# A gated delta-rule layer in chunks of 16 tokens on one core: the first half's errors return in one transfer, its sums are stored in two parts, gates and betas are stored behind them

## What is computed

```python
def step(S, inp):
    qt, kt, vt, at, bt = inp
    err = jnp.einsum('bhij,bhj->bhi', S, kt) - vt
    S = at[..., None] * S - bt[..., None, None] * (err[..., None] * kt[:, :, None, :])
    o = jnp.einsum('bhij,bhj->bhi', S, qt)
    return (S, o)
```

## Time and profile before

| | |
|---|---|
| median of 3 runs | 7554.44 us (7550.18 to 7566.12) |
| the profiled execution | 7551.86 us, span of its instructions 7550.1 us |
| the 64 slots | the first 24 of 40 slices of the span; 56 of them from 508.1 us to 4391.0 us |
| busy in these slots (1500 to 2500 us) | DVE 81%, POOL 72%, PE 63%, ACT 45%, DMA engines 65% |
| the second stage | from about 4570 us on |

### The profile page before, as it was taken

One profiled execution on the slowest core, in us unless ns is written; L12 is line 12 of the kernel. 1 busy time (PEld: TensorE's weight loads), 2 busy tenths in 40 slices (PEclk: granted clock), 3 DMA queues, 4 the chain that ended last, 5 costly groups with the idle time before them and its releaser, 6 DMA issues. The chain is left out here.

```text
span 7550.1 us, 176117 instructions
## 1 busy us (share of the span) xinstructions
PE 5140.1 (68%) x58695; PEld 3396.8 (45%) x58695; DVE 5425.1 (72%) x16005; ACT 3324.8 (44%) x7234; POOL 3635.1 (48%) x4232
## 2 busy tenths in 40 slices
PE   5666666666666666666666643777778777777777
PEld 4554444455554454454454542333433333433333
DVE  6888878888888788878788874555666556665665
ACT  4444444444444444444444432444444444444444
POOL 4777767767767767767767772111111111111110
PEclk8777777777777777777777766888888888888888
DMA  4766666665666666666666651111121111111111
GB/s 118 160 154 140 145 155 134 146 157 133 145 152 138 144 152 139 147 151 138 144 151 140 147 134 50 48 47 45 45 50 45 42 42 42 42 45 42 42 42 35
DMA packets 1172894, 786.82 MB, mean 104 GB/s; under 512 B 1039923, under 2 KB 1091795, under 8 KB 1157844
## 3 DMA queue, kind: packets, MB, share of 16 engines
q1 hardware_dynamic: 864468, 583.96, 34.0%
q10 hardware_dynamic: 307712, 193.48, 10.7%
HBM read 473.80 MB, written 303.50 MB: 103 GB/s over the span
## 5 line engine op out<-in xcount | busy, mean ns | idle before, releaser
L465 POOL TENSOR_TENSOR qp<-qp,pt 128x512 f32<-128x512 f32 (+7 forms) x1024 | 1049.5, 1025 | 85.5 <-issue 5.2
L827 DVE SCALAR_TENSOR_TENSOR p_bank<-y,conv_w,p_bank 128x128 f32<-128x128 f32 x3072 | 826.2, 344 | 241.0 <-ACT p_bank L658 222.2
L524 PE MATMUL p_bank<-st 64*32 64x80 f32 x16384 | 508.3, 292 | 614.4 <-issue 452.8
L460 POOL TENSOR_TENSOR qp<-qp,ab 128x512 f32<-128x512 f32 (+7 forms) x1024 | 864.9, 845 | 75.3
L1684 DVE TENSOR_REDUCE nmax<-w_bank 128x1 f32<-128x512 f32 x1024 | 637.4, 682 | 338.0 <-PE w_bank L1310 330.0
L1265 POOL TENSOR_TENSOR ot<-ot,ln_w 128x1024 f32<-128x1024 f32 x64 | 150.6, 2352 | 1407.5 <-ACT ot L1540 1407.5
L524 PEld LDWEIGHTS p_bank<-st 64*32 64x32 f32 x16384 | 451.8, 142 | 674.4 <-issue 672.4
L462 POOL TENSOR_TENSOR pt<-qp,vb 128x512 f32<-128x512 f32 (+7 forms) x1024 | 747.7, 730 | 9.3 <-DVE vb L904 9.3
L497 PE MATMUL d_bank<-xd,kt 32*64 32x128 f32 x7936 | 366.1, 336 | 407.6 <-DVE st L845 407.6
L594 PEld LDWEIGHTS p_bank<-xnT,wqkv 128*128 128x128 f32 x4096 | 537.7, 213 | 160.4 <-issue 160.4
L594 PE MATMUL p_bank<-xnT,wqkv 128*128 128x128 f32 x4096 | 564.6, 299 | 42.6 <-ACT st L671 36.8
(11 more groups left out here) (219 smaller groups left out, 11695.0 us busy)
## 6 DMA issues: line engine op xcount, KB each, us to landing
db<-decay_dram SPq DMA_DIRECT2D x124, 1024.0 KB, 12.3
prod_dram<-prod ACTq DMA_DIRECT2D x64, 1280.0 KB, 7.4
kp<-prod_dram SPq DMA_DIRECT2D x64, 640.0 KB, 6.2
qp<-prod_dram SPq DMA_DIRECT2D x64, 640.0 KB, 7.7
a_dram<-at ACTq DMA_DIRECT2D x64, 512.0 KB
ab<-a_dram SPq DMA_DIRECT2D x64, 512.0 KB, 6.1
v_dram<-vt ACTq DMA_DIRECT2D x64, 512.0 KB
vb<-v_dram SPq DMA_DIRECT2D x64, 512.0 KB, 5.5
```

What stands on the lines that cost most here:

```text
L460: link(nc.gpsimd.tensor_tensor(q, q, ab[:, g, r:r + 1, :].to_broadcast([128, w, DV]), ALU.mult), 1)
L465: link(nc.gpsimd.tensor_tensor(q, q, pt2[:, 0:w], ALU.add))
L524: mm = nc.tensor.matmul(p_bank[b % 2][at_:at_ + 32, ROW * hq:ROW * hq + ROW], slot_[:, DV:DV + 2 * C], slot_[:, 0:ROW], start=True, stop=True)
L827: nc.vector.scalar_tensor_tensor(out=zz, in0=y[:, j % Y_BANKS, i, :, tap:tap + C], scalar=conv_w[:, m, tap:tap + 1], in1=zz, op0=ALU.mult, ...
```

## The change

Four edits. In DRAM the errors now lie as rows of tokens, and the store of the first half writes 128 x 8 runs of 64 numbers into them; one transfer of 128 rows of 1024 numbers brings the whole chunk back into `xe`, second half included. That second half is never written in the loop; it is filled with zeros once, ahead of the loop, from the cleared tile `vt`, and SP and ACT wait for this. `crossed` stores each of its two banks as soon as it is copied. The stores of gates and betas are taken out of `gates` and `betas` and stand behind `crossed` on ACT.

```diff
@@ -165,7 +165,7 @@
     a_dram = [dram(f"a_dram{g}", [C, GB, H, DV]) for g in range(GROUPS)]
     beta_dram = [dram(f"beta_dram{g}", [GB, H, C]) for g in range(GROUPS)]
     upd_dram = [dram(f"upd_dram{g}", [GB, H, C, DV]) for g in range(GROUPS)]
-    e_dram = [dram(f"e_dram{g}", [GB, H, HALF, DV]) for g in range(GROUPS)]
+    e_dram = [dram(f"e_dram{g}", [C, GB, H, DV]) for g in range(GROUPS)]
     x_dram = [dram(f"x_dram{g}", [C, GB, H, DV]) for g in range(GROUPS)]
     decay_dram = [dram(f"decay_dram{g}", [2, GB * HP, DV]) for g in range(GROUPS)]
     x = ins["L0_attn_x"]
@@ -244,7 +244,7 @@
         def conv_bank(j):
             return (p_bank[0], p_bank[1], c_bank)[j % 3][:]
 
-        consts_in = sem("consts_in")
+        consts_in, e_zeroed = sem("consts_in"), sem("e_zeroed")
         ident_done = sem("ident_done")
         init_done = sem("init_done")
         x_in = [sem(f"x_in{g}") for g in range(GROUPS)]
@@ -288,6 +288,11 @@
                 (conv_b[:], ins["conv_b"]),
             ):
                 sp.dma_start(tile, src).then_inc(consts_in, 16)
+
+            sp.wait_ge(init_done, 1)
+            for g in range(GROUPS):
+                sp.dma_start(e_dram[g].rearrange("t b h i -> b t (h i)"), vt[:]).then_inc(e_zeroed, 16)
+            sp.wait_ge(e_zeroed, 16 * GROUPS)
 
             def load_x(n, g):
                 src = x[GB * g:GB * g + GB].rearrange("b (n t) c -> n b t c", t=C)
@@ -330,19 +335,17 @@
                 if valid(lo, hi):
                     sp.wait_ge(solve_chain, SOLVE_OPS * s + FIRST_HALF_OPS)
                     held(sp, sp_passed)
-                    if due(dma_of(xe_in, n, g, -2, 16 * GB)[1]):
-                        sp.wait_ge(*dma_of(xe_in, n, g, -2, 16 * GB))
+                    if due(dma_of(xe_in, n, g, -2)[1]):
+                        sp.wait_ge(*dma_of(xe_in, n, g, -2))
                         held(sp, sp_passed)
-                    sp.dma_start(e_dram[g].rearrange("b h t i -> (b h) t i"), eb[:, 0:HALF]).then_inc(e_wr[g], 16)
+                    sp.dma_start(e_dram[g][0:HALF].rearrange("t b h i -> (b h) t i"), eb[:, 0:HALF]).then_inc(e_wr[g], 16)
                     sp.wait_ge(*dma_of(v_wr, n, g, 0))
                     held(sp, sp_passed)
                     sp.wait_ge(*dma_of(e_wr, n, g, 0))
                     held(sp, sp_passed)
-                    for b in range(GB):
-                        sp.dma_start(xe[C * b:C * b + HALF].rearrange("t (h i) -> t h i", h=H),
-                                     e_dram[g][b].rearrange("h t i -> t h i")).then_inc(xe_in[g], 16)
+                    sp.dma_start(xe[:], e_dram[g].rearrange("t b h i -> b t (h i)")).then_inc(xe_in[g], 16)
                 if valid(lo, hi):
-                    sp.wait_ge(*dma_of(x_wr, n, g, 0))
+                    sp.wait_ge(*dma_of(x_wr, n, g, 0, 32))
                     held(sp, sp_passed)
                     sp.dma_start(xk[:], x_dram[g].rearrange("t b h i -> (b h) t i")).then_inc(xk_in[g], 16)
                 if updates(lo, hi):
@@ -563,7 +566,7 @@
 
             def cross(s, n, g):
 
-                pe.wait_ge(*dma_of(xe_in, n, g, 0, 16 * GB))
+                pe.wait_ge(*dma_of(xe_in, n, g, 0))
                 pe.wait_ge(f_freed, scores_use(s) + 2)
                 for u in range(2):
                     bank = use(cross_use(s), u)
@@ -636,6 +639,7 @@
         def _(act):
             act.wait_ge(consts_in, 16 * 7)
             act.wait_ge(init_done, 1)
+            act.wait_ge(e_zeroed, 16 * GROUPS)
 
             def filled(first, k):
                 act.wait_ge(f_filled, first + k + 1)
@@ -710,20 +714,21 @@
             def crossed(s, n, g):
 
                 act.wait_ge(*dma_of(p_wr, n, g, 0))
-                if due(dma_of(x_wr, n, g, -1)[1]):
-                    act.wait_ge(*dma_of(x_wr, n, g, -1))
+                if due(dma_of(x_wr, n, g, -1, 32)[1]):
+                    act.wait_ge(*dma_of(x_wr, n, g, -1, 32))
+                if due(dma_of(xk_in, n, g, -2)[1]):
+                    act.wait_ge(*dma_of(xk_in, n, g, -2))
                 for u in range(2):
                     bank = filled(cross_use(s), u)
                     nc.scalar.activation(xo[:, 512 * u:512 * u + 512], bank[:], ACT.Copy).then_inc(f_freed, 1)
-                act.wait_ge(f_freed, cross_use(s) + 2)
-                if due(dma_of(xk_in, n, g, -2)[1]):
-                    act.wait_ge(*dma_of(xk_in, n, g, -2))
-                act.dma_start(x_dram[g].rearrange("t b h i -> b t (h i)"), xo).then_inc(x_wr[g], 16)
+                    act.wait_ge(f_freed, cross_use(s) + u + 1)
+                    dst = x_dram[g][:, :, HP * u:HP * u + HP].rearrange("t b h i -> b t (h i)")
+                    act.dma_start(dst, xo[:, 512 * u:512 * u + 512]).then_inc(x_wr[g], 16)
 
             def products(s, n, g):
-                if due(dma_of(x_wr, n, g, -1)[1]):
+                if due(dma_of(x_wr, n, g, -1, 32)[1]):
                     act.wait_ge(*dma_of(p_wr, n, g, -1))
-                    act.wait_ge(*dma_of(x_wr, n, g, -1))
+                    act.wait_ge(*dma_of(x_wr, n, g, -1, 32))
                 for b in range(GB):
                     act.wait_ge(p_filled, 8 * s + b + 1)
                     nc.scalar.activation(prod[:, b, :], p_bank[b % 2][:, 0:4 * ROW], ACT.Copy).then_inc(p_freed, 1)
@@ -744,6 +749,8 @@
                 for j in range(2):
                     bank = filled(front1_use(s), 1 + j)
                     nc.scalar.activation(at[:, 512 * j:512 * j + 512], bank[:], ACT.Sigmoid).then_inc(f_freed, 1)
+
+            def store_gates(s, n, g):
                 act.wait_ge(f_freed, front1_use(s) + 3)
                 if due(dma_of(ab_in, n, g, -2)[1]):
                     act.wait_ge(*dma_of(ab_in, n, g, -2))
@@ -756,6 +763,8 @@
                 nc.scalar.activation(bt[:], bank[0:H, 0:P], ACT.Sigmoid, bias=bb[:]).then_inc(f_freed, 1)
                 act.wait_ge(f_freed, front1_use(s) + 4)
                 nc.scalar.activation(bt[:], bt[:], ACT.Copy, scale=-1.0).then_inc(bneg_done, 1)
+
+            def store_betas(s, n, g):
                 act.wait_ge(bneg_done, s + 1)
                 if due(dma_of(nb_in, n, g, -2)[1]):
                     act.wait_ge(*dma_of(nb_in, n, g, -2))
@@ -782,6 +791,9 @@
                     place_keys(s + 1, 1 - g)
                 if valid(lo, hi):
                     crossed(s, n, g)
+                if ahead:
+                    store_gates(s + 2, n + 1, g)
+                    store_betas(s + 2, n + 1, g)
                 if front:
                     silu(s + 1, 1 - g, 4)
                     silu(s + 1, 1 - g, 5)
```

## The result

| | before | after |
|---|---|---|
| median | 7557.03 us (7544.2 to 7585.56, 7 runs) | 7515.94 us (7498.94 to 7537.36, 7 runs) |
| ratio of after to before | | 0.9934, 95% interval 0.9916 to 0.9953 |
| span of the profiled execution | 7550.1 us | 7514.1 us |

By the ratio the change makes the kernel 0.66% faster; between the medians it is 41 us, where I forecast 79 (7475). The time lies inside the range of 7395 to 7590.

A forecast was written before the change was run, and what follows sets the result against it. A chain of waits once per slot was taken as the bound, no engine being full. 60 x (-1.1 - 0.4) = -90 and +11 for the start gave -79 us: 7475 us, range 7395 to 7590 for 8 in 10.

The forecast's parts named there:

- Term one: Errors return sooner, so PE's wait for them goes and DVE's for `update` shrinks: -1.1 us per slot, between 0 and -1.8.
- The store, +0.9 us: Errors' store in 1024 runs of 256 B takes 3.0 us instead of 2.1: +0.9 us, between 0 and +2.6.
- The load, 5.5 us: Errors' load as one 512 KB transfer on half of the engines takes 5.5 us, between 4 and 6.5.
- Term two: Sums in two parts bring `db` about 3 us sooner, so `products` gain: -0.4 us per slot, between -1.7 and a loss.
- rival 4: Gates' later store makes `xk` and `db` late by what they won; only the errors' gain stays: 7499 us; chance 0.50.
- Rival 2: `db` catches PE's code fetch earlier, at the start of `products`: +3.3 us in every second slot, 7598 us; chance 0.15.
- a stall split in two: Sign of a wrong forecast: PE's "issue" wait in `products` split in two, or grown above 8 us per slot.
- Rivals 1 and 3: 1: errors no sooner, 7553 us, chance 0.15; 3: `products` end with `db`, 2.8 us sooner, 7397 us, chance 0.15.
- The start, +11 us: Ahead of the loop, the zero fills delay the load of x: +11 us once, between +5 and +13.
- The second half is not the bound: In each slot DVE waits 3.3 us at the convolution after the second half, so `xk` sooner gains nothing there.
- PE waits for its code behind `db`: In `products`, PE's 7.9 us per slot without a shown reason is a wait for code behind `db`'s loads.

The follow-up runs named there:

- the gates back: The whole change, but with the stores of gates and betas at their old place: 7579.73 us, ratio 1.0031 to the kernel before.
- `db` early: Kernel before with gates and betas stored later and both loads of `db` issued ahead of `xk`, behind the errors' load: 7363.33 us, ratio 0.9749.
- `db` late: Kernel before with gates and betas stored later and both loads of `db` at the slot's end, behind the load of `qp`: 7252.43 us, ratio 0.9598.
- the loads split: Kernel before with gates and betas stored later, one load of `db` behind the errors' load, the other behind `qp`: 7223.27 us, ratio 0.9557.
- the last version: Kernel before with gates and betas later, one `db` load ahead of `xk`, one at the slot's end, sums in two parts: 7168.23 us, ratio 0.9487.

## Why the prediction was right, and where its sum was off

**Term one, -1.1 us per slot, held: -1.0** (DVE's wait for `update` 1.79 to 0.79). PE's wait for the errors went, as said. But of the two reasons that I gave, the new transfer and the later gates, only the second is true: alone the late gates take the wait to 0.3, while the single transfer alone takes it to 2.1 (113.6/55), and with the gates back it is 2.9. I had priced the gates' collision with the store at 4.1 us "in the few slots where it happens", and the single load as a gain in all. The store was late in few slots indeed (7 of 51 took over 3 us); what I left out is the gates' collision with the load, which made the errors land at 10.0 us before and at 7.5 without it.

**The store, +0.9 us, was mis-sized: +0.3** (SP's next issue 2.41 us after it in the slot shown, 2.1 before; the median landing of all 56 is 2.3 against 2.0). I had added for runs of 256 B what half of `o_dram`'s store made likely. **The load, 5.5 us, was mis-sized too: 6.9** (9.3 from the store's issue to the landing of the load, less 2.4). The two errors cancel in part: 9.3 us where I had 8.5, and `cross` starts at 9.7. With the gates back it is 11.0.

**Term two, -0.4 us per slot, is the step that failed.** It measured +0.1: from the first to the last matmul of `products` 16.16 us before and 16.25 after (means over 51 and 52 slots), and PE's stall 7.9 and 7.8. I had written that `db` moves 3 us against 1.1 for the start of `products`, and that `products` end with `db`. It was issued 2.3 us sooner, but its last bytes came only 0.7 us sooner: `xk` ahead of it took 7.4 us instead of 6.0, and SP issued the second load of `db` 4.0 us after the first, 1.8 before (means; the slot shown has both in 4.51 us). Both come from the gates' store: with the gates back they are 4.6 and 1.3. That is rival 4.

But the gates' store is not the whole reason. In the run with the parts alone, where it is not in the way of `xk`, `db` was issued 1.0 us and landed 1.4 us sooner and `products` ended 0.1 us sooner. PE stood longer early in `products` (in their first 10 us 1.81 us per slot without a shown reason instead of 0.76) and less long late (5.59 instead of 7.25). So `db` brought forward mostly moved the stall within `products`; that they end with `db` is the premise that failed. 60 x 0.5 = 30 us of the 43 that the sum missed (79 forecast, 36 measured) are in this term.

**Rival 2**, the slower one, came in a small form. After the change PE stands 1.05 us per slot early in `products` instead of 0.76, over 2 us in 6 slots of 52 and in none before, and 7.00 instead of 7.25 late. The rival's condition was met only in part: `db` is issued 0.7 us ahead of the start of `products`, before 0.7 us behind it (means). With gates later and parts the early stall is 1.13 us, with the gates alone 0.70, and `products` end 36.4 instead of 35.2 us after the errors' store: it cost 1.3 us and not 3.3, and kept the parts from gaining there. The price was for every second slot because I took the slot of the earlier trace rows, which has no gap, for one of two kinds. It is the only one of its kind: of the 51 slots of before between 500 and 4100 us, 50 have over 6 us of stall. My sign for this rival, a stall split in two, was no sign, since it was split in 27 of them already. **Rivals 1 and 3** did not come.

**The start, +11 us, held: +12.1.** From the fills' issue at 14.27 us to the next load of x at 23.96 are 9.7 us, 10.2 by the sum.

**The sum.** At 0.85 a slot the 63 would give 53.6 us; the 55 of the stretch gave 46.7 and the other 8, at both ends of the program, 1.3, which makes 48.0. With +12.1 that makes the measured -36. The slot was forecast at 69.1 us and took 69.75. The prediction's own range was not added up from its bounds: it took -1.2 us for term two and +8 for the start, where the bounds that it gives are -1.7 and +5; with these the lower end is 60 x (-1.8 - 1.7) + 5 = -205 and not -172.

**The second half is not the bound**, as I had argued from the convolution's wait: held for this kernel by the parts alone, which took 2.0 us off the wait for `xk` and put 1.9 on the one at the convolution. It ceased to hold once `db` was moved; then the same edit was worth 55 us.

**PE waits for its code behind `db`**: I took it as an inference from one slot. Moving the same loads to two other places took the stall in `products` from 7.6 to 2 us per slot each time. The edits are on SP; PE's program is the same in all of these versions. So that the place of `db` is the cause is shown. A part of the stall moved with it: all that PE stands without a shown reason is 10.2 us per slot with the gates later, 8.4 with `db` early, 7.9 with `db` late and 5.8 with the loads split.

That it is the code that PE waits for is read from all gaps of a trace. In the kernel after, between 500 and 4100 us, `products` have 71 gaps of over 1 us without a shown reason; every one ends 1.2 to 1.8 us after the end of a packet of the instruction queue q8, while these packets are 10.2 us apart in the median. Before it is 70 gaps and 1.3 to 1.8 us, and with `db` early the 47 gaps of `update` have 1.2 to 1.6. The waits at the start of `products`, which DVE's state ends, lie 7.0 us behind the last packet on average. No run moved the code's packets alone.

## What to carry to other kernels

Where the trace shows an engine idle with nothing that it waits for, look at what fills the DMA engines then and at the instruction queue's packets: by these traces a large load that is not urgent starved an engine of its code, and splitting and moving it was worth six times the change studied here (7484.39 to 7223.27 us). Look at many slots before you take one for typical, and after a move at all rows of the engine, since the stall may have gone elsewhere. A store that nobody waits for (the gates) cost time in both places where it met a transfer on the chain; ask of each place which transfer it meets. And an edit that gains nothing may gain once another wait is gone: the sums in two parts came to -16, +10, -2 and -55 us in four neighbourhoods (medians of the versions with and without them; +10 and -2 lie within the intervals).

## What the runs showed of the hardware

**Code behind data.** In the slot of after shown above, the queues from 2081.2 to 2090 us and then from 2090 to 2093.5:

```profile
q1 hardware_dynamic: 287, 1.92, 100.6%
```
```profile
q8 instruction: 1, 0.02, 2.5%
```

In the first stretch `db` fills all engines and no packet of code moves; the block before started at 2079.91, this one at 2090.19, and PE goes on at 2092.95. While `db` moves in this slot, blocks of 16 KB are some 10 us apart; where it does not, as in the slot of the last version, they come 4.3 us apart (1852.21 and 1856.53), with the queues from 1851.8 to 1858 us:

```profile
q1 hardware_dynamic: 1148, 0.39, 25.4%
q8 instruction: 2, 0.03, 2.4%
```

The Trainium skill, "Runtime: NRT & Kernel Launch", section "Instruction fetch mechanics", says that code is refilled in blocks of 16 KiB while the current one runs, and that this is hidden because instructions issue more slowly than blocks come. The block size agrees (0.02 MB in a packet, 16384 bytes in each of the queue's 431); hidden it was not, at 7.8 us per slot by the reading above, and the measurement decides.

**Half of the engines.** The errors' load in one transfer with 8 batches outermost took 6.9 us, as eight transfers of 16 rows 5.7 for the same 512 KB (landing less the store's 2.4 us, means of 52 slots), though the eight issues alone take over 3 us. In every one of the 52 slots the first left 8 packets of 4 bytes in the trace, the second 128, which is 16 for each transfer. The prediction cited a rule for this, of the engines that a shape gives a transfer (the Trainium skill, "DMA: Bandwidth & Descriptors", section "Why a DMA increments its semaphore by 16 and not by 1"); if these packets are the engines' increments of the semaphore, which that section describes, the counts agree with it.

**Short runs.** The store of 256 KB as 1024 runs of 256 B took 2.3 us, as 128 runs of 2 KB 2.0. The Trainium skill, "DMA: Bandwidth & Descriptors", section "Specifications", gives 512 B as the least for full rate; at this size of transfer it cost 0.3 us.

**An issue that waits.** SP's issue of the two loads of `db` took 4.7 us with the gates' store issued 4.7 us ahead of it, and 1.9 with that store at its old place (means of the kernel after and of the run with the gates back). With `db` right ahead of them, the issue of the eight loads of `xd` took 12.0 us instead of 3.8.
